# A gated-attention and routed-experts kernel: row scatters of two batches over five steps in place of four, and the last batch's attention one step sooner

## The chip, the cores and the metric

The kernel runs on one core of one Trainium2 chip. The time is device microseconds for one execution of the whole program; the smaller, the better. The engines are PE (TensorE), DVE (VectorE), ACT (ScalarE), POOL (GpSimd) and SP (SyncE); each runs its own stream of instructions in order, and semaphores tie them together.

## The reference, cut to what matters

```python
x = x + jnp.tanh(g_xattn[0]) * cross_attention(_layernorm(x), ctx_768, ...)   # x: (4, 1024, 256), ctx: (4, 77, 192)
x = x + jnp.tanh(g_ffn[0]) * ffn(_layernorm(x), ...)

def ffn(x, gate_w, gate_b, w1, b1, w2, b2):          # 8 experts, 256 -> 1024 -> 256
    gate_weights = jax.nn.softmax(x @ gate_w + gate_b)
    topk_values, topk_indices = jax.lax.top_k(gate_weights, 2)
    hidden = jax.nn.relu(jnp.einsum('bsd,edh->bseh', x, w1) + b1)
    expert_out = jnp.einsum('bseh,ehd->bsed', hidden, w2) + b2
    sel = jnp.take_along_axis(expert_out, topk_indices[..., None], axis=2)
    return jnp.sum(topk_values[..., None] * sel, axis=2)
```

Each of the 4096 rows goes through attention over 77 context rows and then through the two experts that its gate chooses.

## The kernel before, in words

A row goes only to its two experts. The kernel sorts the rows by expert in a DRAM buffer `xs`: for a batch of 1024 rows it computes the attention, the layer norm and the gate, works out a place in `xs` for each row and choice, and writes the rows there with 16 indirect DMAs from POOL (`scatter_rows`, L579, 128 rows each). Then tiles of 128 rows of one expert, the **slots**, are loaded from `xs` (`load_rows` on SP), multiplied by that expert's weights and added to the output at their rows by one more indirect DMA (`scatter(s)` on POOL, L659). There are S = 71 slots and one **step** of the expert loop for each.

The batches are b = 0 to 3. Attention of b=0 and b=1 runs ahead of the loop. Attention of b=2 and b=3 is laid into the loop, one row tile per step: at step s, batch b is at its own stage j = s - AT[b], for j from 0 to 14 (`attention_steps`). Stages 0 and 1 are the first statistics on DVE (L972), stage 2 has `root_1` on POOL (L601) and PE's first transposes, stages 2 to 10 the attention matmuls, 11 and 12 the second norm and the gate, 13 and 14 the places and the split of the rows into two fp16 parts (`low_rows`, L1217). The row scatters of b begin at stage 15. The table `AT`, the table `CNT` (the step at which the rows of a batch are counted per expert, with the slot tables two steps later and the padding 6 to 15 steps after the last count) and the calls of `share` set all of this by hand.

Each engine walks the steps in its own loop:

- PE, step s: transposes of slot s+2 (L1711), first layer of slot s+1 (L1730 to L1734), attention, second layer of slot s (L1752 to L1754), attention.
- ACT: the transposed rows (L856), bias (L866) and relu (L875) of slot s+1, attention's `xT` copy (L766), the scaled output of slot s (L882).
- DVE: sum (L1407) and low part (L1415) of slot s+1, the finished rows of slot s (L1422), then counts and statistics.
- POOL: `root_1` and other small work of attention, the index copy of slot s+2 (L651), the row scatters (`share`, L579), and at last the output scatter of slot s (L659), which waits for L1422 of that step.
- SP: `load_rows(s)`; the first slot that may hold rows of a batch (25 for b=2, 41 for b=3) waits until all scatters of that batch have landed.

A slot's finished rows stand in three buffers, so L1422 of step s waits for the output scatter of step s-3.

Of the kernel before, what the change touches and what calls it, by code (L numbers as in the profile page):

```python
# [5 lines left out]
def gated_attention_and_routed_experts(  # L6
# [15 lines left out]
    P = 128  # L22
    B, L, D = x.shape
    _, LC, DC = ctx_768.shape
    E, _, H = w1.shape
    KO = 2
    T = L // P
# [11 lines left out]
    SCALE = float(Wq.shape[1]) ** -0.5  # L39
    EB = 2  # L40
    NB = 2
    AT = {2: 1, 3: 18}
    CNT = {1: 0, 2: 14, 3: 31}
    DX, LX = D + E, LC + E
    U = 4
    NHB = NH // 2
# [9 lines left out]
    with ExitStack() as ctx:  # L56
# [357 lines left out]
        def attention_steps(s):  # L414
            return [(b, s - AT[b]) for b in range(NB, B) if 0 <= s - AT[b] <= 14]

# [13 lines left out]
        def _(sp):  # L430
# [25 lines left out]
            def store_x1(b):  # L456

                sp.wait_ge(s_x1, (b + 1) * T)
                if b:
                    sp.wait_ge(s_outd, b * 16)  # L460
                sp.dma_start(tile_tokens(out_rows, b), xb[b % 2][:, :, 0:D]).then_inc(s_outd, 16)

            def next_x(b):

                sp.wait_ge(s_outd, (b + 1) * 16)
                sp.wait_ge(s_x16l, (b + 1) * T)
                load_x(b + 2)
# [41 lines left out]
            for s in range(U, S):  # L509
                load_rows(s)  # L510
                if s == U + 1:
                    next_x(1)
                if s == AT[2] + 14:
                    store_x1(2)
                if s == AT[3] + 14:
                    store_x1(3)
# [5 lines left out]
        def _(pool):  # L522
# [47 lines left out]
            def scatter_rows(b, first, last):  # L570
                for n in range(first, last):
                    k, i = divmod(n, T)
                    if n == 0:
                        pool.wait_ge(s_dest, b + 1)
                        pool.wait_ge(s_gx, b + 1)
                        pool.wait_ge(s_x16h, (b + 1) * T)
                        pool.wait_ge(s_x16l, (b + 1) * T)
                        pool.wait_ge(s_tok, 1 + b + 1)
                    g.indirect_dma_start(out=xs, out_offset=bass.IndirectOffsetOnAxis(ap=dest[:, n:n + 1], axis=0),  # L579
                                         in_=xext[:, i, :], in_offset=None).then_inc(s_scat, 16)  # L580

            def pad_rows():

                pool.wait_ge(s_scat, B * KO * T * 16)
                g.memset(xext[:, 0:2, 0:TC], 0.0).then_inc(s_padz, 1)
                for j in range(2):
                    g.iota(xext[:, j, TC:XW].bitcast(I32), [[0, 1]], base=(B - 1) * L + T - 2 + j,
                           channel_multiplier=T).then_inc(s_padz, 1)

            def scatter_pads(n):  # L590
                j, e = divmod(n, E)
                if n == 0:
                    pool.wait_ge(s_padi, 1)
                    pool.wait_ge(s_padz, 3)
                g.indirect_dma_start(out=xs, out_offset=bass.IndirectOffsetOnAxis(ap=pad_i[:, n:n + 1], axis=0),
                                     in_=xext[:, j, :], in_offset=None, bounds_check=E * N - 1,
                                     oob_is_err=False).then_inc(s_pads, 16)

            def root_1(b):
                pool.wait_ge(s_vv, b + 1)  # L600
                g.tensor_tensor(rs[b % 2][:], vv[b % 2][:], neghalf[:], ALU.pow).then_inc(s_rs, 1)  # L601

            def root_2(b):
                pool.wait_ge(s_vv3, b + 1)
                g.tensor_tensor(rs[b % 2][:], vv[b % 2][:], neghalf[:], ALU.pow).then_inc(s_rs3, 1)

            def rows_norm_2(b, first, last):
                pool.wait_ge(s_rs3, b + 1)
                pool.wait_ge(s_outd, (b + 1) * 16)
                for i in range(first, last):  # L610
                    x = xb[b % 2][:, i, 0:D]
                    g.tensor_scalar(x, x, mv[b % 2][:, i, 0:1], rs[b % 2][:, i:i + 1], ALU.subtract,
                                    ALU.mult).then_inc(s_xn, 1)

            def token_ids(b):
                if b:
                    pool.wait_ge(s_scat, b * KO * T * 16)
                else:
                    pool.wait_ge(s_zst, 16)
                g.tensor_copy(xext[:, :, TC].bitcast(I32), tok[:, b * T:(b + 1) * T]).then_inc(s_tok, 1)  # L620
# [26 lines left out]
            def index(s):  # L647
                pool.wait_ge(g_xg[s % U], (s // U + 1) * 16)
                if s >= U:
                    pool.wait_ge(g_out, (s - U + 1) * 16)  # L650
                g.tensor_copy(idx[s % U][:], xg[s % U][:, TC:XW].bitcast(I32)).then_inc(g_ix, 1)  # L651

            def scatter(s):
                pool.wait_ge(g_ix, s + 1)
                pool.wait_ge(g_y2, s + 1)
                pool.wait_ge(s_outd, min(round_of(s) + 1, B) * 16)
                if s:
                    pool.wait_ge(g_out, s * 16)
                g.indirect_dma_start(out=out_rows,  # L659
                                     out_offset=bass.IndirectOffsetOnAxis(ap=idx[s % U][:, 0:1], axis=0),  # L660
                                     in_=y2[s % 3], in_offset=None, compute_op=ALU.add).then_inc(g_out, 16)
# [3 lines left out]
            def share(b, k, n):  # L665
                if 0 <= k < n:
                    scatter_rows(b, KO * T * k // n, KO * T * (k + 1) // n)

            for s in range(S):
                for b, j in attention_steps(s):  # L670
                    if j == 2:
                        root_1(b)
                    if j == 11:
                        root_2(b)
                    if j in (12, 13):
                        rows_norm_2(b, (j - 12) * T // 2, (j - 11) * T // 2)
                if s + 2 < S:
                    index(s + 2)
                share(1, s, 4)
                share(2, s - AT[2] - 15, 4)  # L680
                share(3, s - AT[3] - 15, 4)
                scatter(s)
                if s == CNT[3] + 7:
                    pad_rows()
                if CNT[3] + 8 <= s < CNT[3] + 8 + E:
                    scatter_pads(2 * (s - CNT[3] - 8))
                    scatter_pads(2 * (s - CNT[3] - 8) + 1)
                for b, j in attention_steps(s):
                    if j == 13:
                        token_ids(b)  # L690
# [211 lines left out]
        def _(dve):  # L902
# [152 lines left out]
            def counts_1(r):  # L1055

                dve.wait_ge(s_cnt, r + 1)
                seg_step(v.tensor_copy(nti[:], counted))
                seg_step(v.tensor_copy(cnt[:], counted))
                seg_wait()  # L1060
                seg_step(v.tensor_scalar(ntj[:], nti[:], P.bit_length() - 1, None, ALU.arith_shift_right))
                seg_wait()
                seg_step(v.tensor_copy(seg_f[r % 2][:], ntj[:]))
                seg_wait()
                if r:
                    dve.wait_ge(s_rowT, r)
                segments_1(seg_f[(r + 1) % 2], seg_f[r % 2])

            def counts_2():
                segments_2()  # L1070
                v.scalar_tensor_tensor(slot_row[:], slot[:], float(P), slot_off[:], ALU.mult, ALU.add).then_inc(s_row, 1)
# [290 lines left out]
            def attention_end(s):  # L1362
# [11 lines left out]
                for r in range(1, B):  # L1374
                    if s == CNT[r]:
                        counts_1(r)
                    if s == CNT[r] + 1:
                        counts_2()
# [430 lines left out]
```

## Time and profile before

| | us |
|---|---|
| median of 3 runs | 634.6 |
| the runs | 632.09, 634.6, 639.15 |
| the profiled execution | 638.39 |
| its span, first to last instruction | 636.7 |

The profile is of one execution. Its views: the page with busy time per engine, 40 slices of the span and the chain that ended last; busy time by stretches; the timeline, which gives each instruction's start, length, and the idle time of its engine before it with what ended it ("issue" where nothing known did); and the waits, by what was waited for. All times are microseconds from the first instruction.

### The profile page before, as it was taken

How to read it: one execution, taken by the hardware profiler on the slowest of the kernel's cores; microseconds unless marked ns; L12 is line 12 of the kernel's file. 1: busy time of each engine (PE TensorE's matmuls, PEld its weight loads, DVE VectorE, ACT ScalarE, POOL GpSimd, SP SyncE). 2: the span in 40 equal slices, each digit the busy share in tenths (PEclk: the TensorE clock that was granted, in tenths of full speed). 3: DMA queues.
4: the chain of work that ended last, by engine and by line, in shares of the span. 5: the costliest groups of instructions: out<-in, count | busy, mean ns of one | idle time of the engine just before them, and what ended most of it. 6: DMA issues, size and time to landing. Idle time of an engine off the chain costs nothing.

```text
span 636.7 us, 15679 instructions
## 1 busy us (share of the span) xinstructions
PE 520.9 (82%) x4723; PEld 430.4 (68%) x4724; DVE 404.2 (63%) x1157; ACT 415.4 (65%) x1061; POOL 271.8 (43%) x288
## 2 busy tenths in 40 slices
PE   6958417508778999987799999877999999999991
PEld 2537206306467887765588877756989999999991
DVE  3268799588376676873466677745755565665650
ACT  2387874656346776754466766646888788888880
POOL 3110228513583223966523238665476622233331
PEclk9585555557799999997899999979999999999997
DMA  6919505824432324134322332333333333333221
GB/s 172 328 39 379 178 0 186 282 71 124 151 86 52 43 36 109 28 79 94 69 44 35 44 83 55 69 85 87 54 72 58 53 53 52 52 53 51 36 27 17
DMA packets 47634, 57.07 MB, mean 90 GB/s; under 512 B 6856, under 2 KB 43198, under 8 KB 47424
## 3 DMA queue, kind: packets, MB, share of 16 engines
q1 hardware_dynamic: 32223, 36.60, 18.7%
q0 software_dynamic: 14064, 18.55, 17.0%
q10 hardware_dynamic: 1264, 0.93, 0.5%
q8 instruction: 40, 0.66, 0.5%
q14 instruction: 43, 0.34, 0.2%
HBM read 33.19 MB, written 24.49 MB: 91 GB/s over the span
## 4 chain that ended last, share of the span: by engine, by line
PE 50%; DVE 18%; issue 12%; ACT 11%; DMA 4%; ACTq 1%; POOL 1%; another core or an unknown queue 1%; DVEq 1%; SPq 0%; POOLq 0%
PE hid L1730 8%; PE hid L1734 7%; PE bank L1754 6%; PE bank L1752 6%; PE bank L1753 6%; PE hid L1731 4%; PE hid L1733 4%; ACT pool L866 4%; DVE pool L1407 3%; DVE w1l L957 2%; DVE w2l L957 2%; PE bank L1711 2%; ACT w2l L727 2%; DMA out_dram<-pool,idx 2%; PE bank L1593 2%
## 5 line engine op out<-in xcount | busy, mean ns | idle before, releaser
L659 POOL DMA_INDIRECT out_dram<-pool,idx x71 | 114.8, 1617 | 229.2 <-DVE pool L1422 186.3
L866 ACT ACTIVATE pool<-hid,b1s 128x128 f32<-128x128 f32 x568 | 166.7, 374 | 53.1 <-remote 29.6
L1730 PE MATMUL hid<-pool,w1h 128*128 128x256 f16 x568 | 158.8, 280 | 8.8 <-DVE pool L1407 5.0
L1752 PE MATMUL bank<-w2h,pool 128*128 x568 | 154.9, 273 | 10.3 <-issue 9.8
L1407 DVE TENSOR_TENSOR pool<-hid,pool 128x512 f32<-128x512 f32 x142 | 96.8, 690 | 101.5 <-ACT pool L866 87.3
L1734 PE MATMUL hid<-pool,w1h 128*128 128x256 f16 x568 | 158.9, 280 | 2.1 <-issue 2.1
L1753 PE MATMUL bank<-w2l,pool 128*128 x568 | 154.8, 273 | 3.1 <-issue 3.1
L1754 PE MATMUL bank<-w2h,pool 128*128 x568 | 154.9, 273 | 0.8 <-issue 0.7
L1731 PE MATMUL hid<-pool,w1l 128*128 128x128 f16 x568 | 126.8, 223 | 2.1 <-issue 2.1
L1733 PE MATMUL hid<-pool,w1l 128*128 128x128 f16 x568 | 127.0, 224 | 1.9 <-issue 1.9
L875 ACT ACTIVATE pool<-pool 128x512 f16<-128x512 f32 x142 | 89.9, 636 | 34.4 <-DVE pool L1407 34.1
L1415 DVE SCALAR_TENSOR_TENSOR pool<-pool 128x512 f16<-128x512 f32 x142 | 95.0, 686 | 5.4
L579 POOL DMA_INDIRECT xs<-xext,dest x64 | 71.1, 1111 | 30.2 <-issue 22.2
L1730 PEld LDWEIGHTS hid<-pool,w1h 128*128 x568 | 56.6, 100 | 18.1 <-issue 16.5
L1752 PEld LDWEIGHTS bank<-w2h,pool 128*128 128x128 f16 x568 | 55.6, 98 | 19.3 <-issue 12.8
L1733 PEld LDWEIGHTS hid<-pool,w1l 128*128 x568 | 56.8, 100 | 12.1 <-issue 4.3
L1753 PEld LDWEIGHTS bank<-w2l,pool 128*128 128x128 f16 x568 | 55.6, 98 | 10.8 <-issue 4.3
L1754 PEld LDWEIGHTS bank<-w2h,pool 128*128 128x128 f16 x568 | 55.6, 98 | 9.6 <-issue 3.3
L1731 PEld LDWEIGHTS hid<-pool,w1l 128*128 x568 | 56.8, 100 | 7.1 <-issue 1.1
L1734 PEld LDWEIGHTS hid<-pool,w1h 128*128 x568 | 56.9, 100 | 3.1 <-issue 3.1
L651 POOL COPY idx<-pool 128x1 int32<-128x1 int32 x71 | 51.1, 721 | 12.6 <-DMA pool<-xs 12.6
L1422 DVE SCALAR_TENSOR_TENSOR pool<-pool,q 128x256 f32<-128x256 f32 x71 | 34.5, 487 | 28.1 <-ACT pool L882 21.5
(257 smaller groups left out, 734.8 us busy)
## 6 DMA issues: line engine op xcount, KB each, us to landing
pool<-in_L_ffn_w_dram SPq DMA_DIRECT2D x12, 1024.0 KB
pool<-xs SPq DMA_DIRECT2D x71, 132.5 KB
xb<-in_x_dram SPq DMA_DIRECT2D x4, 1024.0 KB
out_dram<-xb SPq DMA_DIRECT2D x4, 1024.0 KB, 4.9
out_dram<-pool,idx POOLq DMA_INDIRECT x71
w1h<-in_L_ffn_w_dram SPq DMA_DIRECT2D x1, 1024.0 KB, 4.9
w1l<-in_L_ffn_w_dram SPq DMA_DIRECT2D x1, 1024.0 KB, 7.5
w2h<-in_L_ffn_w_dram SPq DMA_DIRECT2D x1, 1024.0 KB, 9.6
```

The lines of the kernel that those rows point to most:

```text
L659: g.indirect_dma_start(out=out_rows, out_offset=bass.IndirectOffsetOnAxis(ap=idx[s % U][:, 0:1], axis=0), in_=y2[s % 3], in_offset=None, c ...
L866: a.activation(hb[:, c * P:(c + 1) * P], bank[c // 2][:, (2 * (c % 2) + 1) * P:2 * (c % 2 + 1) * P], ACT.Identity, bias=b1s[:, ds(e * NH + ...
L875: a.activation(hh[s % 2][:, half], hb[:, half], ACT.Relu).then_inc(g_hh, 1)
L1407: v.tensor_tensor(part, main, part, ALU.add).then_inc(g_hb, 1)
L1415: v.scalar_tensor_tensor(hl[s % 2][:, half], hb[:, half], 0.0, hh[s % 2][:, half], ALU.max, ALU.subtract).then_inc(g_hl, 1)
L1730: t.matmul(o, wh, xhl, start=True, stop=False)
L1731: t.matmul(o[:, 0:P], wl, xh, start=False, stop=False)
L1733: t.matmul(o[:, 0:P], wl, xh, start=False, stop=False)
L1734: mm = t.matmul(o, wh, xhl, start=False, stop=True)
L1752: t.matmul(o, hh[s % 2][:, hs], wh, start=c == 0, stop=False)
L1753: t.matmul(o, hh[s % 2][:, hs], wl, start=False, stop=False)
L1754: mm = t.matmul(o, hl[s % 2][:, hs], wh, start=False, stop=c == NH - 1)
```

## The change

The shares of b=2 and b=3 are five in place of four: with 16 scatters, 3, 3, 3, 3 and 4 per step. For b=3, `AT` goes from 18 to 17 and `CNT` from 31 to 30, so its attention, counts, tables, padding and scatters all begin one step sooner. Its scatters ran in steps 33 to 36 and now run in 32 to 36; those of b=2 ran in 16 to 19 and now run in 16 to 20. The share of b=1 stays as it is.

```diff
-    AT = {2: 1, 3: 18}
-    CNT = {1: 0, 2: 14, 3: 31}
+    AT = {2: 1, 3: 17}
+    CNT = {1: 0, 2: 14, 3: 30}
@@
                 share(1, s, 4)
-                share(2, s - AT[2] - 15, 4)
-                share(3, s - AT[3] - 15, 4)
+                share(2, s - AT[2] - 15, 5)
+                share(3, s - AT[3] - 15, 5)
                 scatter(s)
```

The program for POOL from step 16 on, before (a step ends with its L659; x4 counts equal rows):

```order
L651 COPY idx<-pool 128x1
L579 DMA xs<-xext,dest 32896x265 x4
L659 DMA out_dram<-pool,idx 4096x256
L651 COPY idx<-pool 128x1
L579 DMA xs<-xext,dest 32896x265 x4
L659 DMA out_dram<-pool,idx 4096x256
L651 COPY idx<-pool 128x1
L579 DMA xs<-xext,dest 32896x265 x4
L659 DMA out_dram<-pool,idx 4096x256
L651 COPY idx<-pool 128x1
L579 DMA xs<-xext,dest 32896x265 x4
L659 DMA out_dram<-pool,idx 4096x256
```

And the same engine now, from step 18 on (steps 16 and 17 are as 18):

```order
L651 COPY idx<-pool 128x1
L579 DMA xs<-xext,dest 32896x265 x3
L659 DMA out_dram<-pool,idx 4096x256
L601 TENSOR_TENSOR rs<-vv,neghalf 128x8
L651 COPY idx<-pool 128x1
L579 DMA xs<-xext,dest 32896x265 x3
L659 DMA out_dram<-pool,idx 4096x256
L651 COPY idx<-pool 128x1
L579 DMA xs<-xext,dest 32896x265 x4
L659 DMA out_dram<-pool,idx 4096x256
```

Each step gives up one scatter, a fifth step takes four, and the `root_1` of b=3 (L601), which had stood in step 20 without a scatter, now stands in step 19 ahead of three.

The attention of b=3 begins on DVE with its first statistics (L972). On DVE around steps 17 and 18, before and now as one piece:

```order
 L1422 ISA
 L1422 SCALAR_TENSOR_TENSOR pool<-pool,q 128x256
-L1394 TENSOR_LOAD exp_tab
-L1394 ISA x2
-L1400 ISA
-L1400 TENSOR_TENSOR q<-pool,inv 128x2
-L1407 TENSOR_TENSOR pool<-hid,pool 128x512 x2
-L1415 SCALAR_TENSOR_TENSOR pool<-pool 128x512 x2
-L1422 ISA
-L1422 SCALAR_TENSOR_TENSOR pool<-pool,q 128x256
 L972 BN_STATS st<-xb 128x6 x4
 L1394 TENSOR_LOAD exp_tab
```

One step's work of the experts, which stood ahead of the statistics, now comes behind them; PE, ACT and SP move in the same way by one step from there to the end of b=3.

## Rows read from the trace of the kernel before

**Rows 1.** The page: span, granted clock by slices, chain, instruction queue q8 (packets, MB, share).

```profile
span 636.7 us, 15679 instructions
...
PEclk9585555557799999997899999979999999999997
...
q8 instruction: 40, 0.66, 0.5%
...
PE 50%; DVE 18%; issue 12%; ACT 11%; DMA 4%; ACTq 1%; POOL 1%; another core or an unknown queue 1%; DVEq 1%; SPq 0%; POOLq 0%
```

**Rows 2.** One line's instructions, L1422: count, least/median/most ns, first and last start.

```profile
L1422 DVE SCALAR_TENSOR_TENSOR pool<-pool,q x71: 471/485/686, 159.2 to 624.9; 128x256 f32<-128x256 f32 x71
```

**Rows 3.** Busy time by stretches: borders, length, busy us per engine, clock, DMA, GB/s.

```profile
180.04:188.26 8.22, 5.12 (x46) 3.89 (x45) 6.33 (x25) 4.29 (x13) 7.09 (x7) 1.00 0.37 89
188.26:196.92 8.66, 6.78 (x69) 5.63 (x69) 3.94 (x11) 4.98 (x15) 3.83 (x4) 1.00 0.41 94
275.82:283.07 7.25, 5.80 (x59) 4.57 (x57) 6.28 (x14) 4.26 (x13) 5.23 (x5) 1.00 0.28 48
283.07:294.35 11.28, 7.42 (x56) 4.70 (x55) 3.99 (x11) 4.38 (x13) 7.58 (x8) 0.79 0.43 116
294.35:301.81 7.46, 7.42 (x70) 6.33 (x69) 3.32 (x6) 4.50 (x13) 5.12 (x6) 0.85 0.37 72
301.81:313.59 11.78, 8.23 (x60) 5.62 (x60) 4.44 (x10) 4.59 (x13) 6.66 (x7) 0.86 0.31 83
...
313.59:326.46 12.87, 11.36 (x112) 9.95 (x111) 9.41 (x31) 9.02 (x28) 5.26 (x5) 1.00 0.30 53
...
340.48:368.66 28.18, 27.89 (x278) 24.39 (x278) 19.34 (x53) 19.51 (x60) 7.06 (x8) 1.00 0.24 35
...
411.72:422.97 11.25, 7.02 (x57) 4.46 (x56) 4.08 (x12) 4.39 (x13) 7.58 (x8) 0.84 0.41 112
422.97:430.46 7.49, 7.49 (x66) 6.50 (x65) 4.79 (x16) 4.37 (x12) 5.16 (x6) 0.78 0.31 57
430.46:440.83 10.37, 6.84 (x67) 5.06 (x65) 4.99 (x18) 4.87 (x13) 6.60 (x7) 1.00 0.34 93
...
456.57:495.43 38.86, 38.79 (x423) 35.09 (x421) 23.24 (x42) 31.18 (x85) 27.28 (x27) 1.00 0.36 64
539.39:594.36 54.97, 54.97 (x603) 50.17 (x601) 33.19 (x61) 45.80 (x121) 17.59 (x20) 1.00 0.32 52
```

**Rows 4.** Timeline of PE in step 17: start, length, instruction, idle before it.

```profile
286.85 0.27 PE L1752 MATMUL bank<-w2h,pool 128*128 x1 [0.33 <-issue]
...
293.51 0.28 PE L1733 MATMUL hid<-pool,w1l 128*128 128x128 f16 x1 [0.46 <-issue]
```

**Rows 5.** Waits in step 17: who for whom, us in total, times, longest.

```profile
ACT pool L866 <- remote: 5.5, 2, 3.8
DVE pool L1407 <- issue: 5.4, 1, 5.4
```

**Rows 6.** Timeline of POOL in steps 16 and 17.

```profile
285.56 1.60 POOL L659 DMA_INDIRECT out_dram<-pool,idx  x1 [0.30 <-issue]
...
290.10 0.97 POOL L579 DMA_INDIRECT xs<-xext,dest  x1 [0.30 <-issue]
291.37 0.97 POOL L579 DMA_INDIRECT xs<-xext,dest  x1 [0.30 <-issue]
```

**Rows 7.** DMA queues in step 17 (283.07 to 294.35): packets, MB, share.

```profile
q8 instruction: 1, 0.02, 0.9%
```

**Rows 8.** Timeline of POOL behind the L1422 of step 34.

```profile
424.21 1.61 POOL L659 DMA_INDIRECT out_dram<-pool,idx  x1 [3.22 <-issue]
```

**Rows 9.** Timeline of ACT in step 4.

```profile
191.58 0.62 ACT L866 ACTIVATE pool<-hid,b1s 128x128 f32<-128x128 f32 x2 [1.32 <-PE hid L1734]
```

**Rows 10.** Waits of SP, 300 to 330 us.

```profile
SPq L499 <- DMA xs<-xext,dest: 7.9, 1, 7.9
```

**Rows 11.** Timeline of PE where it turns slot 25.

```profile
333.82 0.39 PE L1711 MATMUL bank<-ident,pool 128*128 128x128 f16 x4
```

## The prediction

> **What bounds the kernel now.** I read four views, in this order. The page comes first [rows 1]: in a span of 636.7 us PE takes half of the chain that ended last, but 12% of that chain is "issue", time in which an engine waits for nothing that the profile names. The reader should also see the clock line: the expert loop runs at full clock but for a few slices in the middle.
>
> The second view cuts the loop by steps. Each step ends with one `L1422` on DVE (the sum that finishes a slot's rows), 71 in all [rows 2]; I took their start times as borders and asked for the busy time between them [rows 3]. Below, step s is the stretch that ends with the start of its `L1422`. A plain step late in the loop takes 5.50 us (54.97 for ten) with PE never idle. A step with attention of b=2 or b=3 takes 7.05 (28.18 for four). The steps that hold the row scatters (`L579`) of b=2 and b=3 are very different, and they alternate: 7.25, 11.28, 7.46, 11.78 us for steps 16 to 19; step 33 is as 16, and steps 34 to 36 take 11.25, 7.49, 10.37. There is no attention matmul in any of these, so against 5.50 the eight steps lose 74.1 - 44.0 = 30 us, and four **long steps** (17, 19, 34, 36) hold 44.7 - 22.0 = 22.7 of it.
>
> The third view is one long step, 17, instruction by instruction. PE runs a few matmuls, then stands still for a third to half a microsecond, again and again from 286.5 to 293.5, always "issue" [rows 4] (the first and the last of eight such rows); DVE stands 5.4 us and ACT 5.5 us behind it [rows 5]. In the same 7 us GpSimd is without a pause: an output scatter at 285.56, an index copy, four row scatters up to 292.3 [rows 6]. So PE's stall begins about a microsecond after GpSimd's run begins and ends about a microsecond after the last scatter. Steps 19, 34 and 36 show the same. The clock adds to it: it is at its lower level (1.2 GHz) for part of steps 17, 18, 19, 34 and 35, granted 0.79, 0.85, 0.86, 0.84 and 0.78 [rows 3], each time after PE has stood in such a stall.
>
> Why every second step? In step 17 one packet of 0.02 MB is recorded on the instruction queue q8, which by its count I take for PE's code [rows 7]; in step 18 none, in step 19 one, and over the program 40 of 0.66 MB in all [rows 1]. So a stall seems to need two things together: PE comes to a new piece of its code, and GpSimd is in a burst of scatters. That is my reading of the coincidence, not something a row states. The Trainium skill, "Runtime: NRT & Kernel Launch", section "Instruction fetch mechanics", describes code that streams in 16 KiB blocks by a DMA queue of the engine's own and calls the cost of a boundary mostly hidden. By that rule the bursts would not matter to PE and the terms (a) and (b) below would be zero; the trace agrees for the plain steps and speaks against it for the four long ones.
>
> **The change part by part.** The 16 scatters of a batch now come as 3, 3, 3, 3, 4 in steps 16 to 20 and, because b=3 begins a step sooner, in steps 32 to 36. Nothing is added or taken away; 32 row scatters stand in other places.
>
> (a) *Shorter bursts in long steps.* PE's code before step 19 is in the same order, and from step 34 on the same count of instructions stands ahead, so its fetches should fall into steps 17, 19, 34 and 36 again. Three of these now hold three scatters, the last still four. One scatter takes 1.27 us from start to start (290.10, 291.37) [rows 6]. If the stall lasts as long as the burst, that is 3 x 1.27 = 3.8 us. Bounds: 0, if a stall's length is that of the fetch alone; if a long step becomes as its short neighbour, 4.3 us for it (11.78 - 7.46).
>
> (b) *Bursts on time.* In step 16 GpSimd cannot start the output scatter before 285.56, 2.49 us after `L1422` (283.07), because its own four row scatters stand ahead of it; where GpSimd is free, it starts 1.24 us after (424.21 against 422.97) [rows 8]. With three it is on time, and the burst of step 17 begins and ends 1.2 us sooner. The same in steps 33 and 34. PE enters its new code at the same moment as before, so some of the shift shortens the stall: I take half, 2 x 0.6 = 1.2 us; bounds 0 and 2.5.
>
> (c) *Clock.* The five grants make 4.7 + 2.2 + 3.3 + 3.6 + 3.3 = 17.1 us at half rate. Where this lies inside a stall it costs nothing; in steps 18 and 35 PE is busy throughout, and there it costs half of 5.5, 2.8 us, and 1 to 1.5 more in 19 and 34. Shorter stalls may leave the clock up; I take a third, 1.5 us; bounds 0 and 4.
>
> (d) *Attention of b=3 over the bursts.* Its steps j=2 and j=3 move from 20 and 21, which had no scatter, to 19 and 20, which have three and four. On POOL the `pow` of `root_1` (L601) now stands ahead of three scatters. The nearest rows are those of b=2, whose j=2 and j=3 are steps 3 and 4, with b=1's last four scatters in step 3: 8.22 and 8.66 us, 16.88 together, against 12.87 for steps 20 and 21, so 4.0 us more [rows 3]. In step 4 ACT stood 1.32 us before `L866` [rows 9]. But part of this pays for waits that step 19 has anyway: PE's wait for ACT's `xT` copy, which comes with each attention step, can lie in a stall. I take +1.5; bounds 0 and +4.0.
>
> (e) *At nothing.* SP's load of slot 25 waits for the last scatter of b=2: 7.9 us in SP's view of waits [rows 10], until the end of step 19 (313.6). It will go out about one step later, near 320. PE turns that slot at 333.82 [rows 11], so some 13 us of cover remain; were it gone, each microsecond late would be one on the path. Slot 41 waits for b=3's last scatter, which stays in step 36. One fewer attention step at the end (32) and one more at the start (17) leave the sum of attention steps equal; DVE's `low_rows` moves with them, from 32 to 31. The counting, tables and the 16 pad scatters come a step sooner; around the latter, steps take 38.86 / 7 = 5.55 us, within 0.05 of plain ones [rows 3]. The lateness of POOL in step 19 costs nothing by itself: the sum of a step waits for the output scatter three before it.
>
> Sum: -3.8 - 1.2 - 1.5 + 1.5 = **-5.0 us**. The profiled execution took 638.4 (span 636.7 and 1.7 around it), so 633.4; the median of the three runs is 634.6, 3.8 below it, and on that scale I predict **629.6 us**.
>
> **The rivals.**
> 1. *No net gain.* A long step's stall has its own length whatever the burst, or one of the fifth bursts makes one more long step. (a) to (c) are then 0 or eaten: +1.5 leaves 636.1, one more long step (+5) brings the forecast to 634.6. For it: PE's pauses in the stall are of equal length, some 0.7 us from start to start, as if something were fetched piece by piece, not as if it waited for a burst's end. Against: begin and end follow GpSimd's run in all four.
> 2. *A long step falls away.* For it: step 3 had a burst, a packet on q8 and the `pow` between, and no long stall (8.22 us); step 19 gets just this `pow` now. Then 11.78 becomes some 7.5, 4.3 instead of 1.3 of gain: -8.0, so 626.6; with two such, 623.6.
> 3. *The fifth bursts stall, and it is slower.* In step 20 and in step 32 PE, or ACT ahead of it, crosses into new code during the added burst. Each makes a plain step (5.5) into one of 10.4 to 11.3, say +5.4, and the step after it slower by the clock, +1: 12.8 for both, less 5.0, gives +7.8, 642.4. One alone gives only rival 1; it needs both. For it: five bursts are a wider target than four, and code fetches of the other engines also fall there. Against: before, PE's fetches fell every second step, and steps 16, 18, 33 and 35 had bursts of four without a stall.
>
> **How the numbers follow.** Forecast 0.40 (own range 626 to 633), rival 1 0.22, rival 2 0.25, rival 3 0.13. One per cent, 6.3 us, is about what a measurement can tell here: the three runs shown lie 7 us apart. Faster by more needs less than 628.3: a third of the forecast's share (0.13) and rival 2, together 0.38. Slower by more is rival 3, 0.13. The rest, 0.49, is within 1%. The range goes from 621, past two vanished stalls, to 639, short of rival 3.
>
> **What would show it.** (a): long steps 17, 19 and 34 at 9 to 10.5 us in place of 11.3 to 11.8, PE's "issue" pauses ending a microsecond after the third scatter; wrong if they still last 7 us. (b): the output scatter 1.25 us after `L1422` in steps 16 and 33. (c): fewer than 17 us at the lower clock. (d): steps 19 to 21 and ACT's waits in them; wrong if step 20 takes 10 us. Rival 3 shows as a new long step at 20 or 32. The prediction is wrong as a whole if the stalls do not follow the scatters: then the long steps could move anywhere, or stay.

## The result, and the profile after

The changed kernel takes 626.67 us, the median of four runs (623.66 to 628.30); the kernel before, run beside it, 636.09 (632.09 to 639.15). The ratio is 0.985, with a 95% interval of 0.981 to 0.990: 9.4 us, 1.5%, faster. The profiled execution took 623.66 us, the fastest of the four, where that of the kernel before took 638.39, so the two profiles lie further apart than the medians. Here and below, ratios leave out single runs that were slow as a whole (one of e1's, at 632.44 us, the profiled one of e2's, at 638.27, and one of the kernel before, at 2777.40), while medians and ranges keep them.

The page of the changed kernel: span and instructions, granted clock in 40 slices, and the chain that ended last.

```profile
span 621.9 us, 15679 instructions
...
PEclk8976555557999999999999999999999999999996
...
PE 48%; DVE 17%; issue 11%; ACT 9%; DMA 6%; SPq 2%; POOL 2%; ACTq 1%; another core or an unknown queue 1%; DVEq 1%; POOLq 0%
```

Against [rows 1], the instructions are the same in number, "issue" in the chain is 11% for 12%, and the clock line has no dip left in the middle of the program.

The changed kernel by stretches, cut at `L1422` as in [rows 3] (borders, length, busy us of PE, weight loads, DVE, ACT and POOL, clock, DMA share, GB/s). These are steps 17 to 21, and then 33, 34, 36 and 37:

```profile
279.68:287.90 8.22, 6.36 (x64) 4.96 (x62) 3.93 (x11) 4.27 (x13) 6.14 (x6) 1.00 0.47 123
287.90:292.57 4.67, 4.46 (x48) 4.12 (x49) 4.46 (x11) 4.30 (x13) 2.95 (x4) 1.00 0.28 27
292.57:300.86 8.29, 6.15 (x57) 4.66 (x55) 5.44 (x22) 4.36 (x13) 7.20 (x7) 1.00 0.41 102
300.86:311.05 10.19, 8.09 (x85) 7.04 (x84) 4.00 (x10) 5.20 (x15) 7.16 (x8) 1.00 0.34 94
311.05:317.91 6.86, 5.86 (x56) 4.74 (x54) 4.84 (x14) 4.78 (x15) 1.80 (x2) 1.00 0.39 81
...
396.31:404.56 8.25, 6.42 (x64) 4.90 (x62) 3.93 (x12) 4.28 (x13) 6.12 (x6) 1.00 0.44 120
404.56:410.15 5.59, 5.41 (x59) 4.92 (x60) 4.62 (x16) 4.35 (x13) 3.87 (x4) 1.00 0.36 69
...
417.31:423.21 5.90, 5.90 (x66) 5.24 (x65) 3.82 (x11) 4.27 (x13) 4.11 (x6) 1.00 0.34 72
423.21:431.46 8.25, 6.31 (x67) 5.00 (x64) 4.34 (x13) 4.26 (x13) 3.68 (x4) 1.00 0.42 101
```

The two profiled executions, summed over the same steps:

| steps | before, us | after, us | difference |
|---|---|---|---|
| up to the `L1422` of step 15 | 275.8 | 272.4 | -3.4 |
| 16 to 18 | 26.0 | 20.1 | -5.9 |
| 19 | 11.8 | 8.3 | -3.5 |
| 20 and 21 | 12.9 | 17.1 | +4.2 |
| 22 to 31 | 71.5 | 71.2 | -0.4 |
| 32 to 37 | 47.6 | 42.4 | -5.2 |
| 38 to the end of the span | 191.1 | 190.5 | -0.6 |

The first row holds the same program in both kernels, so its 3.4 us are not the change's: nearly half of it (1.5) stands before step 0 has ended, and most of the rest in step 1 (14.44 and 12.27 us), which e1, e2 and e4 show at 12.3 to 12.4 and so does e3, the kernel before with an edit at its head. What the change does lies in steps 16 to 37: 169.7 us before, 159.0 after. e3 and e4 below repeat it with 169.1 and 158.9. The two sums, -10.7 and -10.2, agree with the 9.4 of the medians within what the runs leave open.

PE in step 17 of the changed kernel, by the timeline (start, length, instruction, idle time before it). These are its only "issue" pauses from step 17 to the end of step 18:

```profile
284.21 0.27 PE L1752 MATMUL bank<-w2h,pool 128*128 x1 [0.76 <-issue]
...
288.12 0.27 PE L1730 MATMUL hid<-pool,w1h 128*128 128x256 f16 x1 [1.17 <-issue]
```

Before, step 17 alone has nine, of 0.16 to 0.65 us ([rows 4] show the first and the last). POOL in the same steps:

```profile
280.93 1.60 POOL L659 DMA_INDIRECT out_dram<-pool,idx  x1 [0.32 <-issue]
...
289.15 1.60 POOL L659 DMA_INDIRECT out_dram<-pool,idx  x1 [2.24 <-issue]
...
295.01 1.60 POOL L659 DMA_INDIRECT out_dram<-pool,idx  x1 [0.30 <-issue]
296.04 2.29 POOL L601 TENSOR_TENSOR rs<-vv,neghalf 128x8 f32<-128x8 f32 x1
```

The output scatter of step 16 starts 1.25 us after `L1422` (280.93 against 279.68), on time; the three row scatters of step 17 are over before 287, and POOL then stands 2.24 us. From 289.15 on it has no pause, and `root_1` of b=3 follows the output scatter that is 2.44 us behind its `L1422`.

Where the change costs is step 20, with attention and the burst of four in one step. PE's longest wait in it (instruction, what it waited for, total, times, longest):

```profile
PE bank L1593 <- ACT xT L766: 2.1, 1, 2.1
```

PE waits for ACT's `xT` copy, ACT for PE's first layer (1.12 us before `L866`) and for something the profile can't name (1.40 us of "remote" before `L882`; [rows 5] have "remote" too). Of the stall's sign, an "issue" pause of PE, step 20 has none.

### The profile page after: what moved, and what is told of

It reads as the page before. It is cut to its first block, busy times and chain, and to the rows that moved or that the text cites. A ratio compares the mean times of both kernels' runs of the same rounds, so it can differ in the third digit from the quotient of the medians.

```text
span 621.9 us, 15679 instructions
## 1 busy us (share of the span) xinstructions
PE 506.0 (81%) x4723; PEld 422.2 (68%) x4724; DVE 402.7 (65%) x1157; ACT 414.6 (67%) x1061; POOL 273.1 (44%) x288
## 3 DMA queue, kind: packets, MB, share of 16 engines
q0 software_dynamic: 14064, 18.55, 17.1%
## 4 chain that ended last, share of the span: by engine, by line
PE 48%; DVE 17%; issue 11%; ACT 9%; DMA 6%; SPq 2%; POOL 2%; ACTq 1%; another core or an unknown queue 1%; DVEq 1%; POOLq 0%
PE hid L1730 8%; PE hid L1734 8%; PE bank L1752 7%; PE bank L1753 6%; PE bank L1754 6%; ACT pool L866 4%; PE hid L1733 4%; PE hid L1731 4%; DMA out_dram<-pool,idx 3%; DVE pool L1407 2%; DMA xb<-in_x_dram 2%; DVE w1l L957 2%; DVE w2l L957 2%; PE bank L1711 2%; PE bank L1593 1%
## 5 line engine op out<-in xcount | busy, mean ns | idle before, releaser
L659 POOL DMA_INDIRECT out_dram<-pool,idx x71 | 114.8, 1617 | 215.2 <-DVE pool L1422 181.2
L866 ACT ACTIVATE pool<-hid,b1s 128x128 f32<-128x128 f32 x568 | 166.5, 373 | 40.6 <-remote 19.1
L1730 PE MATMUL hid<-pool,w1h 128*128 128x256 f16 x568 | 156.2, 275 | 10.5 <-DVE pool L1407 4.7
L1734 PE MATMUL hid<-pool,w1h 128*128 128x256 f16 x568 | 156.4, 275 | 0.0
L1733 PE MATMUL hid<-pool,w1l 128*128 128x128 f16 x568 | 125.3, 221 | 0.8 <-issue 0.8
L1731 PE MATMUL hid<-pool,w1l 128*128 128x128 f16 x568 | 125.3, 221 | 0.7 <-issue 0.7
L579 POOL DMA_INDIRECT xs<-xext,dest x64 | 72.5, 1132 | 29.9 <-issue 22.0
L1730 PEld LDWEIGHTS hid<-pool,w1h 128*128 x568 | 55.9, 98 | 19.6 <-issue 17.8
L1733 PEld LDWEIGHTS hid<-pool,w1l 128*128 x568 | 56.0, 99 | 7.5 <-issue 0.6
L1731 PEld LDWEIGHTS hid<-pool,w1l 128*128 x568 | 56.0, 99 | 7.4 <-issue 2.1
L651 POOL COPY idx<-pool 128x1 int32<-128x1 int32 x71 | 52.7, 743 | 12.5 <-DMA pool<-xs 12.5
L1734 PEld LDWEIGHTS hid<-pool,w1h 128*128 x568 | 56.0, 99 | 0.6 <-issue 0.6
L1422 DVE SCALAR_TENSOR_TENSOR pool<-pool,q 128x256 f32<-128x256 f32 x71 | 34.3, 484 | 30.1 <-ACT pool L882 23.6
```

The costliest lines, as they stand in the source:

```text
L659: g.indirect_dma_start(out=out_rows, out_offset=bass.IndirectOffsetOnAxis(ap=idx[s % U][:, 0:1], axis=0), in_=y2[s % 3], in_offset=None, c ...
L866: a.activation(hb[:, c * P:(c + 1) * P], bank[c // 2][:, (2 * (c % 2) + 1) * P:2 * (c % 2 + 1) * P], ACT.Identity, bias=b1s[:, ds(e * NH + ...
L1730: t.matmul(o, wh, xhl, start=True, stop=False)
L1731: t.matmul(o[:, 0:P], wl, xh, start=False, stop=False)
L1733: t.matmul(o[:, 0:P], wl, xh, start=False, stop=False)
L1734: mm = t.matmul(o, wh, xhl, start=False, stop=True)
```

## The experiments

Three readings were set against each other. The *code reading*, that of the prediction: a stall needs a burst of scatters and a new piece of PE's code together. The *burst reading*: the burst alone makes it, by its length. The *unbroken-run reading*: POOL without a pause, however it is filled, makes it. The twelve kernels ran in three groups, each group beside the kernel before on one chip. Groups 2 and 3 landed on other chips than group 1, and this mattered more than anything else: the kernel before takes 634.93 us in group 1 (median of 19 runs), and 610.13 in both later groups. Below, the "first chip" is that of group 1; the result above has no chip on record, but its 636.09 us are of that kind.

### e1: five shares alone

```diff
-                share(2, s - AT[2] - 15, 4)
-                share(3, s - AT[3] - 15, 4)
+                share(2, s - AT[2] - 15, 5)
+                share(3, s - AT[3] - 15, 5)
```

> One part of the change alone: both batches spread over five steps (3, 3, 3, 3, 4), but the attention of the last batch stays at its old step; its scatters run in steps 33 to 37. Theory A (the length of GpSimd's burst makes the PE stalls): this part carries nearly all of the gain; no step with PE standing for 6 to 7 us in bursts of three, PE at the full clock in steps 17 to 19 and 34 to 36, 624 to 629 us, 7 to 11 us under the kernel before. Theory B (the gain comes from the sooner start of the last batch, the split gives nothing): within 2 us of the kernel before, long steps of 11 us at 17, 19, 34 and 36 as before.

Measured: 626.24 us (622.79 to 632.44), ratio 0.989 (0.984 to 0.995). Steps 17 to 19, 21 and 37 of e1:

```profile
281.26:289.49 8.23, 7.23 (x76) 5.91 (x75) 3.96 (x11) 4.27 (x13) 6.09 (x6) 1.00 0.48 126
289.49:294.06 4.57, 4.22 (x46) 3.62 (x43) 3.24 (x7) 4.28 (x13) 3.15 (x3) 1.00 0.30 24
294.06:300.03 5.97, 5.97 (x68) 5.34 (x65) 4.41 (x12) 4.17 (x13) 4.89 (x6) 1.00 0.48 114
...
306.23:315.97 9.74, 8.72 (x90) 7.36 (x90) 4.03 (x11) 4.88 (x15) 7.61 (x8) 1.00 0.29 73
...
419.00:429.48 10.48, 8.05 (x75) 5.95 (x73) 3.80 (x10) 4.32 (x12) 8.35 (x9) 0.98 0.38 98
```

Step 19 has three scatters and no attention, and it takes 5.97 us with PE busy in all of it; before it took 11.78. POOL has no pause there, nor anywhere from 290.74 to 315.23, which speaks against the unbroken-run reading. Its timeline around that step:

```profile
292.71 1.48 POOL L579 DMA_INDIRECT xs<-xext,dest  x1 [0.17 <-issue]
294.50 0.97 POOL L579 DMA_INDIRECT xs<-xext,dest  x1 [0.31 <-issue]
295.78 0.97 POOL L579 DMA_INDIRECT xs<-xext,dest  x1 [0.30 <-issue]
297.05 1.61 POOL L659 DMA_INDIRECT out_dram<-pool,idx  x1 [0.30 <-issue]
```

The bursts of four, which POOL reaches in steps 21 and 37, are again the long steps, and in 37 PE has six of the pauses. The five shares alone give the whole gain, as far as the runs can tell: the median is within 0.4 us of the changed kernel's, and the interval of the ratio reaches from 3 to 10 us.

### e2: the sooner start alone

```diff
-    AT = {2: 1, 3: 18}
-    CNT = {1: 0, 2: 14, 3: 31}
+    AT = {2: 1, 3: 17}
+    CNT = {1: 0, 2: 14, 3: 30}
```

> The other part alone: attention, counts and scatters of the last batch one step sooner, but four scatters in each of four steps (16 to 19 and 32 to 35). Theory A: long stalls stay in step 17 and 19, and two more in steps 33 to 35; no gain, 634 to 640 us. Theory B: the whole gain, 624 to 629 us.

Measured: 632.59 us (627.69 to 638.27), ratio 0.996 (0.993 to 0.999). Its profiled execution is its slowest (638.27 us), so only the places of the long steps are read from it. Steps 17, 19 and 33:

```profile
283.48:294.52 11.04, 8.49 (x63) 6.23 (x62) 3.99 (x11) 4.39 (x13) 7.86 (x8) 0.81 0.43 117
...
300.46:309.00 8.54, 5.82 (x55) 4.62 (x53) 5.44 (x20) 4.66 (x13) 7.41 (x7) 1.00 0.33 84
...
403.33:414.31 10.98, 7.76 (x64) 5.36 (x61) 3.99 (x11) 4.28 (x13) 7.81 (x8) 0.92 0.42 116
```

Four scatters in a step, and the long step is back; b=3's first one has moved with its scatters from step 34 to 33, and behind it steps 34 to 36 take 7.27, 7.85 and 9.26. Under the code reading, with PE's code from step 34 on at its old place, it should have stayed at 34. But step 19, with four scatters behind the `pow` of b=3's `root_1`, takes only 8.54 us for 11.78, with two "issue" pauses: four scatters don't always make a long step. The start one step sooner gives 2.3 us here. Beside the five shares it gives nothing that the medians can tell (e1 626.24, e4 below 626.49, changed kernel 626.67), and by the profiles it costs: steps 16 to 38 take 161.2 us in e1, 164.0 in the changed kernel and in e4, 175.2 before, and the 2.8 more than in e1 come from steps 19 to 21 (21.9 against 25.3).

### e3 and e4: PE's code moved against the scatters

```diff
             warm(20)
+            for _ in range(64):
+                t.matmul(bank[3][:, 0:1], ones16[:], ones16[:, 0:1], start=True, stop=True)
```

This adds 64 matmuls of one column to PE's warm-up, in the kernel before (e3) and in the changed one (e4), and moves all later code of PE against the borders of its pieces.

> The kernel before with 64 one-column matmuls (128 PE instructions, half of a 16 KB piece of code) added while PE waits for its first weights; they write a PSUM column that is overwritten. In every later step the packets on q8 should be recorded one step earlier. Theory 1 (a stall needs a new piece of PE code and a burst together): the long steps move from 17, 19, 34, 36 to their neighbours 16, 18, 33, 35. Theory 2 (a stall needs only GpSimd's unbroken run, whatever PE's code): long steps stay at 17, 19, 34, 36. Time within 5 us of the kernel before by both.

Measured: 636.28 us (632.82 to 638.02), ratio 1.000 (0.998 to 1.003). Its steps 17 to 19 and 36:

```profile
281.79:292.73 10.94, 8.41 (x64) 5.22 (x62) 4.00 (x11) 4.39 (x13) 7.78 (x8) 0.84 0.43 120
292.73:299.42 6.69, 6.03 (x53) 5.13 (x53) 3.32 (x7) 4.23 (x12) 4.65 (x5) 0.76 0.41 83
299.42:310.34 10.92, 7.95 (x70) 5.65 (x68) 4.46 (x11) 4.88 (x13) 6.97 (x8) 0.97 0.32 87
...
425.70:438.58 12.88, 9.80 (x74) 6.33 (x72) 4.99 (x17) 4.88 (x13) 7.48 (x8) 0.90 0.31 90
```

The only instruction queue with a packet in e3's step 19 (packets, MB, share; q8 has none), and the last of PE's pauses there:

```profile
q14 instruction: 1, 0.01, 0.4%
```

```profile
308.98 0.22 PE L1735 MATMUL hid<-pool,w1l 128*128 128x128 f16 x1 [0.93 <-issue]
```

Step 19 is as long as ever, with the same pauses, and no q8 packet lies in it; nor does one in step 36. Step 18 has one (0.02 MB) and is a short step. The long steps don't follow PE's code: the code reading has fallen.

With it falls its reason why the long steps come every second time, though steps 16, 18, 33 and 35 of the kernel before have four scatters too. POOL's timeline there, the output scatters of steps 15, 17 and 18:

```profile
277.06 2.90 POOL L659 DMA_INDIRECT out_dram<-pool,idx  x1 [4.22 <-DVE pool L1422]
...
295.61 1.59 POOL L659 DMA_INDIRECT out_dram<-pool,idx  x1 [3.27 <-issue]
...
303.06 1.60 POOL L659 DMA_INDIRECT out_dram<-pool,idx  x1 [0.30 <-issue]
```

POOL does not begin anew in step 17: it has had no pause since 277.06, and its run of eight row scatters lasts until 292.3. The next run of eight goes from 295.61 to 309.9. In each of the four such runs (277.06, 295.61, 405.71, 424.21) the first half lies in the short step, PE's pauses begin 8.1 to 9.5 us into the run, and the long step that they make lets POOL catch up and stand 3 to 5 us. Read so, the alternation is that of POOL falling behind and catching up; no run moved the start of a POOL run alone to try it. A long run alone is not the cause either: e1's from 290.74 has ten row scatters in 24.5 us, three a step at first, and PE's pauses in it sum to 1.3 us. What these four long steps share is four scatters a step, a second time in a row. Where four come behind threes (e1's steps 21 and 37), the step is long too, but PE's pauses in it sum to 1.0 and 2.2 us, against 3.4 to 4.1 in the four.

> The changed kernel with the same 64 small matmuls at its start. Theory 1: PE's code pieces now fall into other steps, among them the four-scatter steps 20 and 36; one or two long stalls come back, 630 to 636 us. Theory 2: no long stall, as in the changed kernel, 624 to 629 us.

Measured: 626.49 us (623.77 to 628.01), ratio 0.987 (0.985 to 0.990). Steps 17, 19 and 20 take 8.20, 8.31 and 10.21 us, and 36 and 37 5.31 and 8.40: nearly as in the changed kernel, with the code elsewhere.

### e5, e6, e11: scatters where nothing else goes on

The changed kernel, with extra row scatters into a spare buffer laid into plain steps late in the loop: `n` of them in a step, with so many rows and columns, ahead of the output scatter (`place` 0) or behind it (1). The text of the edit, with the table of e5:

```diff
+    JUNK = {47: (3, 128, 265, 0), ...}   # 47-50: 3 a step, 54-57: 4, 61-64: 5
+            def extra(s, place):
+                if s in JUNK and JUNK[s][3] == place:
+                    ...
+                    for _ in range(n):
+                        g.indirect_dma_start(out=to, out_offset=bass.IndirectOffsetOnAxis(ap=tok[0:rows, i:i + 1], axis=0),
+                                             in_=xext[0:rows, i, 0:cols], in_offset=None).then_inc(s_junk, 16)
...
+                extra(s, 0)
                 scatter(s)
+                extra(s, 1)
```

> The changed kernel with extra row scatters into scratch DRAM in plain steps without attention or real row scatters: three per step in steps 47 to 50, four in 54 to 57, five in 61 to 64 (each of 128 rows, ahead of the step's output scatter); the result is untouched. GpSimd's own work per step would be about 5.9, 7.1 and 8.4 us. Theory of a threshold (a stall of PE needs four or more in one burst): steps with three take 5.5 to 6.5 us and PE never stands; with four and five every second step takes 10 to 12 us with PE pausing at 0.7 us spacing. Rival, GpSimd's rate alone: 5.9, 7.1, 8.4 us per step, no PE pauses. Rival, a stall grows evenly with the scatters: steps with three already take 8 us or more.

Measured, one run: 621.23 us. A step of e5 with three extra scatters and one with five, steps 49 and 64:

```profile
472.43:477.92 5.49, 5.49 (x63) 5.03 (x61) 3.40 (x7) 4.62 (x13) 4.42 (x6) 1.00 0.32 104
...
557.18:562.67 5.49, 5.49 (x62) 4.83 (x60) 3.32 (x7) 4.60 (x13) 4.27 (x5) 1.00 0.39 125
```

No dose makes PE stand: its "issue" pauses are four, of at most 0.26 us, in 120 us. All twelve steps take 5.48 to 6.02 us, while POOL falls behind; its output scatters come late, and the bill is paid behind the bursts, in steps 66 and 67, where DVE waits 7.0 us for output scatters (7.57 and 8.48 us).

> The same with four extra scatters per step, changed in kind: in steps 47 to 50 each of 64 rows (half the rows and bytes), in 54 to 57 of 128 rows but 512 bytes a row (half the bytes, same rows), in 61 to 64 full ones but placed behind the output scatter instead of ahead of it. If the bytes make the stall, both of the first groups are free of it; if the number of rows (descriptors), only the first; if the number of GpSimd's DMA instructions in a run, neither (10 us steps in both). Behind the output scatter: by the unbroken run there is no difference from ahead of it (10 to 12 us every second step); if it is the lateness of the output scatter that matters, no stall.

Measured, one run: 615.19 us (four extra scatters a step: of 64 rows in 47 to 50, of 128 columns in 54 to 57, behind the output scatter in 61 to 64). All steps with them take 4.57 to 5.58 us, and PE has not one "issue" pause from 450 us to 575. Here too POOL's backlog is paid for later: steps 60 and 66 to 68 take 6.9 to 7.0 us.

> The changed kernel with extra scatters into scratch DRAM in plain steps: three per step in steps 47 to 50, four in 54 to 57, four of only 64 rows in 61 to 64. On a 635 us chip, by the threshold: PE pauses of 0.7 us spacing and steps of 8 to 11 us in the second group, none in the first; in the third group pauses only if the number of instructions counts and not their rows. On a 610 us chip: no pauses in any group, steps of 5.5 to 6.

Measured, one run: 617.67 us (three, four, and four of 64 rows). Steps 48 to 50, with three, take 6.10, 6.29 and 6.18, those with four 5.50 to 5.78, those with 64 rows 5.49 to 5.59; PE has six single "issue" pauses of 0.17 to 0.34 us in 120 us, no row of them. These three kernels were to measure the stall by its dose. They ran on the two chips on which the kernel before takes 610.13 us. On the one of them where it was profiled it has no stall either (e9), and on the other e5's own step 1 has none (5.80 us), so these kernels don't say what the dose does where there is one.

### e9 and e10: both kernels again on another chip

Unchanged kernels: e9 is the kernel before, e10 the changed one.

> The kernel before, unchanged, with a profile on this chip. On the chip of the second group of runs it took 610 us, on the first 635. If the long steps are a property of some chips: where it takes 635, steps 17, 19, 34 and 36 are 10 to 13 us long with PE pauses and half clock; where it takes 610, the same bursts of four stand there and those steps take 5 to 8 us with no pauses. If the chips differ in something else, the long steps are there on both.

Measured: 611.31 us in its one run, and 610.13 (607.67 to 611.75) as the median of the runs beside the group. Its steps 17 to 19, then 21 and 39:

```profile
273.29:278.07 4.78, 4.74 (x52) 4.17 (x50) 3.81 (x11) 4.14 (x13) 4.01 (x5) 1.00 0.35 105
278.07:283.81 5.74, 5.64 (x63) 5.00 (x61) 3.33 (x8) 4.59 (x13) 4.52 (x5) 1.00 0.53 139
283.81:289.38 5.57, 5.57 (x63) 4.88 (x61) 4.44 (x11) 4.54 (x13) 4.49 (x6) 1.00 0.50 101
...
295.58:308.00 12.42, 8.69 (x71) 7.06 (x71) 4.04 (x10) 4.88 (x15) 7.02 (x7) 0.86 0.40 80
...
421.02:429.43 8.41, 6.60 (x72) 5.81 (x73) 4.27 (x13) 4.88 (x13) 3.97 (x7) 1.00 0.45 85
```

The same program, with the same bursts of four: steps 17 and 19 take 4.78 and 5.57 us, not 11.28 and 11.78, though each has its q8 packet. But step 21 has gone from 6.67 to 12.42. The timeline there shows why:

```profile
297.93 1.59 POOL L659 DMA_INDIRECT out_dram<-pool,idx  x1 [0.30 <-issue]
298.95 2.29 POOL L601 TENSOR_TENSOR rs<-vv,neghalf 128x8 f32<-128x8 f32 x1
...
301.34 0.30 DVE L1172 SCALAR_TENSOR_TENSOR pr<-bank,rs,cst 128x77 f32<-128x77 f32 x1 [5.27 <-POOL rs L601]
```

POOL needs four row scatters, an output scatter and an index copy a step, about 7.4 us from one output scatter to the next, and the steps give it 5.6. It falls behind by the burst (the output scatter of step 19 starts at 297.93, 8.55 us after its `L1422`, where a free POOL needs 1.24), so the `pow` of `root_1` comes late, DVE waits 5.27 us for it and PE 3.65 behind that. In step 39 it is a load: the waits there, and SP's from 400 to 440 us.

```profile
PE bank L1711 <- DMA pool<-xs: 2.4, 1, 2.4
```

```profile
SPq L499 <- DMA xs<-xext,dest: 17.9, 1, 17.9
```

Slot 41's rows come late, since b=3's last scatter was.

> The changed kernel, unchanged. Where the kernel before takes 635: 624 to 629 us, as in the result. Where it takes 610: only the terms without a stall are left, GpSimd on time and the attention over the bursts; 602 to 608 us, a gain of 4 to 8, since the changed kernel with extra scatters on that chip ran 619.5 us of span with 16.8 more in its last part.

Measured: 600.13 us (599.34 to 600.73), ratio 0.984 (0.980 to 0.987), 10.0 us faster. Its steps 20, 21 and 39:

```profile
286.87:293.67 6.80, 6.48 (x69) 5.72 (x69) 4.03 (x10) 4.79 (x15) 5.71 (x7) 1.00 0.23 68
293.67:301.00 7.33, 7.33 (x72) 6.26 (x72) 4.84 (x14) 4.94 (x15) 5.88 (x7) 1.00 0.35 94
...
412.92:419.06 6.14, 5.92 (x65) 5.26 (x65) 3.31 (x6) 4.63 (x13) 3.63 (x7) 1.00 0.43 78
```

By the medians the gain is as large as on the first chip, above the 4 to 8 us expected, and it stands elsewhere. Of the 10.6 us between the spans of the two profiled executions (609.6 and 599.0), 3.2 lie ahead of step 16, in the same program; 4.9 in steps 16 to 37 (149.3 to 144.4), where DVE waits only 0.5 us for `root_1`; 2.4 in 38 to 45, where slot 41 comes nearly in time. So the profiles show 7.3 us that are the change's.

### e7, e8, e12: more of the same

e7 spreads b=1, b=2 and b=3 over six steps each; e8 leaves b=2 and b=3 as changed and spreads b=1 over five; e12 is e8 once more, beside e10.

```diff
-                share(1, s, 4)
+                share(1, s, 5)
```

> The changed kernel with six steps for all three batches in the loop (2, 3, 3, 2, 3, 3: no burst of four left), the scatters of the second batch too. By the threshold: steps 20, 37 and 1 lose their 10, 8 and 12 us and go to 6 to 8; 6 to 10 us under the changed kernel, 617 to 621 us. If five steps had spread enough: 625 to 628 us. If slot 25 or 41 now comes too late: a PE wait for a DMA at step 23 or 39, 628 or more.

Measured: 604.47 us (603.39 to 607.85), ratio 0.992 (0.989 to 0.994). Its step 39, and SP's waits from 390 to 430 us:

```profile
411.08:422.99 11.91, 9.22 (x72) 7.81 (x73) 3.32 (x7) 4.88 (x13) 4.40 (x8) 0.71 0.44 92
```

```profile
SPq L499 <- DMA xs<-xext,dest: 18.9, 1, 18.9
```

Up to step 37 it is as e10 (405.3 and 407.3 us at that `L1422`, where e8 has 405.5). Then step 39 takes 11.91 for e10's 6.14: the last scatter of b=3 has moved one step later, to step 37, slot 41 comes late, and PE stands 3.4 us for it, in a step whose granted clock is 0.71. This is the third outcome that was expected. One share more in the same window is one too many.

> The changed kernel with five steps for the second batch as well (3, 3, 3, 3, 4 in steps 0 to 4). By the threshold: step 1 falls from 12 us to 8 to 9, but the four of step 4 meet the attention of the third batch; 621 to 625 us. If only the total matters: 625 to 628 us.

Measured: 599.37 us (597.62 to 600.72), ratio 0.982 (0.978 to 0.987).

> The changed kernel with five steps for the second batch too, which took 599.4 us on the 610 us chip. On a 635 us chip, by the threshold: step 1 falls from 12 us to about 8, 620 to 625 us. On a 610 us chip: 598 to 601 us again, 4 to 5 under the changed kernel in the same group.

Measured: 598.66 us (597.25 to 599.46), ratio 0.981 (0.977 to 0.984), against 600.13 for the changed kernel in the same group. Its step 4:

```profile
175.40:181.95 6.55, 6.52 (x67) 5.69 (x65) 3.94 (x11) 4.88 (x15) 5.35 (x6) 1.00 0.36 82
```

Step 4 takes 6.55 us for e10's 7.97, and 1.5 us lie between the medians, where 4 to 5 were expected. It is the fastest version, by little if at all: the two sets of four runs overlap (597.25 to 599.46, and 599.34 to 600.73). On the first kind of chip it was not run; there step 1 takes 12 to 14 us for 5.8 here, so more could be had.

## Why the prediction was right, and where its steps were wrong

The forecast was 629.6 us, 5.0 less than before, in a range of 621 to 639. Measured, beside the kernel before: 626.7, 9.4 less. The direction and the range hold; it is more than the forecast, near rival 2. That shorter bursts on POOL shorten PE's stalls was right; that the number came so near is in part luck, since two errors went against each other (the sum, below).

- **The reading of the stall was half wrong.** The stalls do follow the bursts: with three scatters nearly all is gone (8.22 and 4.67 us in steps 17 and 18, against 11.28 and 7.46, with one pause in each), and where four are left or put, long steps are back (21 and 37 in e1, 17 and 33 in e2), though not in every step with four (19 in e2, 16 and 18 before). But the second condition, that PE must come to new code, fell with e3: steps 19 and 36 are long without a q8 packet. The prediction let POOL's run begin at 285.56, a microsecond ahead of the stall; it had begun at 277.06, and this, not the code, goes with every second step. The rule of the Trainium skill, "Runtime: NRT & Kernel Launch", section "Instruction fetch mechanics", that a boundary's cost is mostly hidden, holds in these runs (e3 at 1.000, e9 with packets and no stall); what I drew from it, that the bursts then cost PE nothing, does not hold on the first chip.
- **(a), shorter bursts in long steps, -3.8: too small.** It took the stall to be as long as the burst, so a quarter shorter. In its place the stall drops away between four scatters and three. Step 17 falls by 3.1 us and step 18 by 2.8 behind it, step 19 by 3.5 with the attention moved into it and by 5.8 without (e1); steps 34 and 36 fall by 5.7 and 4.5, of which 33, with b=3's second burst, and 37, in which POOL works off the last, take back 1.0 and 3.5. Steps 17 and 18 together give 5.9, above the second bound of (a), 4.3 for a long step that becomes as its neighbour, since the neighbour got shorter too. The expected 9 to 10.5 us for the long steps was missed downwards.
- **(b), bursts on time, -1.2: seen, not priced.** The output scatter of step 16 starts 1.25 us after `L1422`, as said. What it is worth can't be taken apart from (a).
- **(c), clock, -1.5: too small.** The five grants made 17.1 us at the lower clock before; after, the granted clock is 1.00 from step 16 to step 37. Steps 17 and 18 together lose 5.9 us, of which the vanished stall and the clock can't be separated; the half rate in step 18 is in it, an estimated 1.1 us (half of 2.2), as the forecast's 2.8 are for steps 18 and 35 together. I took a third of the clock's cost where the whole came back. In e4 steps 17 and 20 had 0.86 and 0.91 all the same, at the same length and without an "issue" pause, so the lower clock is not what makes these steps long, and it does not come behind a stall alone.
- **(d), attention of b=3 over the bursts, +1.5: too small.** Steps 20 and 21 cost 4.2 more (12.87 to 17.05), just above the upper bound of 4.0 from the row of b=2, and step 20 takes 10.19 us, which the prediction had named as the sign of (d) being wrong. I took less, since the waits were to hide in a stall that step 19 has anyway; there was no stall in it any more to hide in. And two things stand in the 4.2: e1, whose attention has not moved, takes 15.94 us in these two steps, so 3.1 of it are the fifth burst's, for which the forecast had no term, and 1.1 the attention's. Step 19 pays on top, 8.29 for e1's 5.97, of which the attention itself is an estimated 1.5 (7.05 to 5.50 [rows 3]). The sooner start alone thus costs 3.4 in steps 19 to 21.
- **(e), at nothing: right on this chip only.** Steps 38 on take nearly the same there (191.1 and 190.5). On the faster chips the lateness of POOL is not free: the kernel before pays it in step 21 and step 39, and e7 loses 5 us to one step more of it. "The lateness of POOL costs nothing by itself" left out `root_1` and slot 41's load.
- **The sum.** Measured by steps: -5.9 (16 to 18), -3.5 (19), +4.2 (20 and 21), -5.2 (32 to 37). Gains of 14.6 against the forecast's 6.5 for (a) to (c), a loss of 4.2 against 1.5: two errors of opposite sign, 8.1 and 2.7 us, that partly cancel.
- **Rivals.** The first (no gain) fell; its pauses "of equal length" are of 0.16 to 0.65 us, only their spacing of some 0.7 us is even. The second (a long step falls away) came true in outcome and mostly not for its reason: step 17 has no `pow` in it, and step 19 is short in e1 without one. But e2's step 19, with four scatters behind the `pow`, is 8.54 us long, as that rival would have it. The third was right that the fifth burst hurts in step 20 (10.19 us), though with no "issue" pause of PE, so not as the stall that it meant, and wrong for step 32 (7.25, as step 33 was before). One alone is not a loss, as it said.

What stays open is the mechanism of the stall. On the first chip a second burst of four row scatters, close behind a first, goes with pauses of PE some 0.7 us apart for 6 to 7 us; one behind bursts of three goes with fewer and shorter pauses, and bursts of three alone with one or two or none. Whether it is the count, the rate, or the data in flight, no run here shows, because the three kernels made for it met chips without stalls.

## What to carry to other kernels

Asynchronous work that one engine issues in bursts should be spread until that engine keeps up with the step it lies in: here 16 scatters in five steps instead of four gave 1.5 and 1.6% on two kinds of chip, for two different reasons, and six steps (with those of b=1) lost nearly half of it, as the consumer of the last one came too late. Before a stall is explained by something that coincides with it, move that thing alone (64 tiny matmuls did it here) and see whether the stall follows. When two changes go in together, run each alone: here one of the two gave the gain, and the other 2.3 us by itself and nothing beside the first. And take a hidden lateness as hidden only after listing everything queued behind it on its engine.

## What was not expected of the hardware

The same program takes 634.9 us on one chip and 610.1 on two others, with 631.18 to 638.38 and 607.67 to 611.75 as the lowest and highest of the runs (19, and 7 of group 3). Each chip was used in one group only, so no run tells the chip from the occasion. The 20 us between the profiled executions in steps 16 to 37 (169.7 and 149.3), and the 8.6 in step 1 (14.44 and 5.81), lie where PE stalls beside bursts of four scatters on the first chip, at the lower clock in part; on the faster chips no such stall was seen, even with five in a step (e5). The two rows of step 1, of the kernel before on the first chip and of e9:

```profile
159.17:173.61 14.44, 9.85 (x71) 6.33 (x69) 4.86 (x17) 4.48 (x13) 8.53 (x9) 0.77 0.54 166
```

```profile
158.72:164.53 5.81, 5.64 (x62) 4.88 (x60) 4.68 (x18) 4.59 (x13) 4.90 (x5) 1.00 0.80 277
```

The step without a stall moves its data at 277 GB/s, the one with it at 166, so on the faster chip even the higher rate doesn't make PE stand; for the first chip this says nothing. A kernel tuned on one of them can be bound elsewhere on the other.
